# Fetching one gathered tile in eighteen row by row, from SyncE's and ScalarE's queues

## The reference

```python
def _batchnorm(x, gamma, beta):
    mu = jnp.mean(x, axis=0)
    var = jnp.var(x, axis=0)
    return (x - mu) * jax.lax.rsqrt(var + BN_EPS) * gamma + beta

def _gin_conv(x, src, dst, n, W1, b1, gamma, beta, W2, b2):
    agg = jax.ops.segment_sum(x[src], dst, num_segments=n)
    h = x + agg
    h = jax.nn.relu(_batchnorm(h @ W1 + b1, gamma, beta))
    return jax.nn.relu(h @ W2 + b2)
...
h = jnp.maximum(_layernorm(x, axis=-1), 0.0)      # the input of the network
h = _batchnorm(h, g0, b0)
h = _gin_conv(h, src, dst, n, W1a, b1a, g1, bt1, W1b, b1b)
h = jax.nn.relu(h)
h = _gin_conv(h, src, dst, n, W2a, b2a, g2, bt2, W2b, b2b)
return x + jax.nn.relu(h)
```

## Time and profile before

| | |
|---|---|
| median of 3 runs | 3099.09 us (3087.79 to 3099.72) |
| the profiled execution, its time | 3089.35 us |
| its span, first to last instruction | 3087.5 us |
| PE busy | 2466.4 us, 80% |
| POOL busy | 1827.8 us, 59% |
| DVE busy | 1767.5 us, 57% |
| ACT busy | 450.5 us, 15% |
| gathers on POOL | 1908, 946 ns each |
| mean granted TensorE clock | 0.925 |

### The profile page before, as it was taken

How to read it: one execution, slowest core, us unless ns; L and a number is a source line. 1 busy time by engine, 2 the same in 40 slices (tenths; PEclk the granted TensorE clock), 3 DMA queues, 4 the chain that set the end, 5 groups by cost and what they waited for, 6 DMA issues and landing times.

```text
span 3087.5 us, 30879 instructions
## 1 busy us (share of the span) xinstructions
PE 2466.4 (80%) x10965; PEld 1989.1 (64%) x10965; DVE 1767.5 (57%) x3146; ACT 450.5 (15%) x1311; POOL 1827.8 (59%) x1931
## 2 busy tenths in 40 slices
PE   0086007999999999999998969988888888888888
PEld 0085006777777777777776738877777676777766
DVE  5999984554555444555545745554444444444457
ACT  8745004000000000000002930000000000000037
POOL 2000007777777777777773077777777777777730
PEclk8557558999999999999999969999999999999999
DMA  6582007777777777777774999877777777777758
GB/s 209 186 276 63 0 0 239 247 249 248 252 252 250 246 248 248 248 252 252 248 248 157 328 280 320 302 247 247 248 249 252 251 248 247 248 248 250 252 189 255
DMA packets 262079, 716.17 MB, mean 232 GB/s; under 512 B 38334, under 2 KB 129098, under 8 KB 261918
## 3 DMA queue, kind: packets, MB, share of 16 engines
q0 software_dynamic: 159424, 592.77, 59.3%
q1 hardware_dynamic: 102494, 121.33, 12.1%
HBM read 621.27 MB, written 92.69 MB: 231 GB/s over the span
## 4 chain that ended last, share of the span: by engine, by line
PE 43%; DMA 24%; DVE 15%; POOL 10%; issue 6%; ACT 1%; SPq 0%; DVEq 0%; ACTq 0%; POOLq 0%
PE agg_ps L655 36%; DMA rows<-node_rows,src_all 22%; POOL rows L573 10%; DVE work L1022 5%; DVE work L1023 5%; PE mm_ps L697 3%; PE mm_ps L779 2%; PE mm_ps L701 2%; DMA rows<-in_x 1%; ACT acc L889 1%; DVE work L1452 1%; DVE acc L1458 0%; DMA work<-in_src 0%; PE tr_ps L680 0%; DVE rows L1066 0%
## 5 line engine op out<-in xcount | busy, mean ns | idle before, releaser
L573 POOL DMA_INDIRECT rows<-node_rows,src_all x1908 | 1805.8, 946 | 1128.8 <-issue 545.4
L655 PE MATMUL agg_ps<-rows,work 128*128 128x257 f32 (+1 forms) x8056 | 1874.1, 387 | 243.3 <-DMA rows<-node_rows,src_all 239.3
L655 PEld LDWEIGHTS agg_ps<-rows,work 128*128 128x128 f32 x8056 | 1501.8, 191 | 593.3 <-DMA rows<-node_rows,src_all 220.0
L1291 DVE SCALAR_TENSOR_TENSOR acc<-agg_ps,in_first,acc 128x256 f32 (+1 forms) x230 | 111.5, 485 | 1185.2 <-PE agg_ps L655 1182.9
L1236 DVE TENSOR_TENSOR work<-code_all,lane_ps 128x1536 f32<-128x1536 f32 x212 | 369.7, 1744 | 1.1 <-issue 1.1
L845 ACT ACTIVATE bn_root<-bn_var 128x2 f32<-128x2 f32 x3 | 0.6, 200 | 2300.7 <-DVE bn_var L1202 2300.7
L697 PE MATMUL mm_ps<-sum_major,w_a 128*128 128x256 f32 x784 | 198.5, 386 | 2.1 <-DVE sum_major L1306 1.3
L779 PE MATMUL mm_ps<-w_b,work 128*128 128x256 f32 x784 | 176.4, 387 | 28.0 <-ACT work L901 17.4
L779 PEld LDWEIGHTS mm_ps<-w_b,work 128*128 128x128 f32 x784 | 139.9, 193 | 64.5 <-ACT work L901 30.6
L697 PEld LDWEIGHTS mm_ps<-sum_major,w_a 128*128 128x128 f32 x784 | 144.7, 190 | 36.6 <-issue 16.3
L901 ACT ACTIVATE work<-acc,bn_shift,bn_scale 128x128 f32<-128x128 f32 x392 | 165.8, 484 | 15.2 <-PE mm_ps L779 11.2
(11 more groups left out here) (235 smaller groups left out, 1376.8 us busy)
## 6 DMA issues: line engine op xcount, KB each, us to landing
node_rows<-acc SPq DMA_DIRECT2D x141, 260.0 KB, 4.7
rows<-node_rows,src_all POOLq DMA_INDIRECT x1908, 4.4
node_rows<-acc SPq DMA_DIRECT2D x27, 910.0 KB, 4.1
node_rows<-acc SPq DMA_DIRECT2D x126, 130.0 KB, 4.3
acc<-in_x SPq DMA_DIRECT2D x13, 896.0 KB, 11.0
rows<-in_x SPq DMA_DIRECT2D x13, 896.0 KB, 7.1
out<-acc SPq DMA_DIRECT2D x13, 896.0 KB
acc<-in_x SPq DMA_DIRECT2D x1, 768.0 KB
```

Of the source, the lines that this page charges most:

```text
L573: pool.indirect_dma_start(tile_rows(k, 0, ROWS_OF[t] * DP), None, tables[layer][0:NPOS if layer and g < TWICE and t >= LAST_PAIRED else TA ...
L655: mm = pe.matmul(bank[:, 0:width], hot[:, unit * P:(unit + 1) * P], tile_rows(k, row, width), start=(start and n == 0), stop=(stop and n = ...
L1291: dve.scalar_tensor_tensor(to, agg_ps[g % 2][:, 0:width], lanes[:, g:g + 1], to, ALU.mult, ALU.add).then_inc(sums_added, 1)
```

## The change

In every second edge row (the odd ones, from row 7 in layer 0 and from row 19 in layer 1) tile 8 is no longer gathered by POOL. It is fetched by 128 DMAs of one table row each: lanes 0 to 63 are issued by SP, lanes 64 to 127 by ACT. That is 50 tiles in layer 0 and 44 in layer 1. Each DMA is preceded by the loading of its row number into a register from the new buffer `row_src`, in which DVE stores the numbers of tile 8 at set-up (one operation more). Before the first DMA of a tile the queue waits, as POOL does, for `tiles_done`. The fetched tiles are counted in four semaphores of their own, `row_landed`; the gathered ones use the 24 as before, numbered among themselves. The placing of tiles and the order of PE's and DVE's work are unchanged.

```diff
+ROW_TILE = T - 1
+FIRST_BY_ROWS = 7
+QUEUE_ROWS = P // 2
+ROW_LANDINGS = 4
+
+def by_rows(layer, g, t):
+    return t == ROW_TILE and g % 2 == 1 and g >= (TWICE if layer else FIRST_BY_ROWS)
...
+GATHERED = [k for k, tile in enumerate(TILES) if not by_rows(*tile)]
+FETCHED = [k for k, tile in enumerate(TILES) if by_rows(*tile)]
+GATHER_OF = {k: n for n, k in enumerate(GATHERED)}
+FETCH_OF = {k: n for n, k in enumerate(FETCHED)}
...
+        row_src = sb("row_src", [P, P], I32)
...
+        def wait_landed(engine, k):
+
+            if k in FETCH_OF:
+                n = FETCH_OF[k]
+                engine.wait_ge(row_landed[n % ROW_LANDINGS], 16 * P * (n // ROW_LANDINGS + 1))
+            else:
+                n = GATHER_OF[k]
+                engine.wait_ge(tile_landed[n % LANDINGS], 16 * (n // LANDINGS + 1))
...
+            def fetch_rows(layer):
+
+                sp.wait_ge(walk_ready, 1)
+                sp.wait_ge(first_stored, FIRST_DMAS[layer])
+                sp.wait_ge(table_stored, TABLE_DMAS[layer])
+                for k in FETCHED:
+                    if TILES[k][0] == layer:
+                        g = TILES[k][1]
+                        sp.wait_ge(tiles_done, TILE_BEFORE[k] + 1)
+                        for lane in range(0 * QUEUE_ROWS, (0 + 1) * QUEUE_ROWS):
+                            place = sp.value_load(row_src[g:g + 1, lane:lane + 1], min_val=0, max_val=NPOS - 1)
+                            sp.dma_start(rows[lane:lane + 1, TILE_AT[k] * DP:(TILE_AT[k] + 1) * DP],
+                                         tables[layer][bass.ds(place, 1), :]
+                                         ).then_inc(row_landed[FETCH_OF[k] % ROW_LANDINGS], 16)
+
+            fetch_rows(0)
             copies = copies_of(1)
...
             for to, of, stored in copies:
                 sp.dma_start(to, of).then_inc(stored, 16)
+            fetch_rows(1)
             sp.wait_ge(walks_done, 2)
...
                     for t in tiles_of(layer, g):
-                        gather(layer, g, t)
+                        if not by_rows(layer, g, t):
+                            gather(layer, g, t)
...
                     k = NUMBER[layer, g, t]
-                    pe.wait_ge(tile_landed[k % LANDINGS], landed(k))
+                    wait_landed(pe, k)
...
             def dense(layer):
                 add_self(layer)
                 if layer == 0:
                     bn_root_of(0)
                     act.wait_ge(consts_loaded, 16 * CONST_DMAS)
+                fetch_rows(layer)
                 bn_root_of(layer + 1)
...
+            step(dve.tensor_scalar(row_src[:, :], place_ints[:, ROW_TILE * P:(ROW_TILE + 1) * P], -float(UP), NPOS - 1.0,
+                                   ALU.add, ALU.min))
```

More of the change, by code:

```diff
@@ L306, in build @@
         tile_landed = [sem(f"tile_landed{i}") for i in range(LANDINGS)]
+        row_landed = [sem(f"row_landed{i}") for i in range(ROW_LANDINGS)]
         hot_begun = sem("hot_begun")
@@ L372, in tile_rows, with last_users @@
             return rows[:, at_row:at_row + width]
[L374 to L378, removed]
+        def wait_landed(engine, k):
[5 more added lines that the diff above has]
+                engine.wait_ge(tile_landed[n % LANDINGS], 16 * (n // LANDINGS + 1))
+        def last_users(layer):
+            own = [k for k in GATHERED if k < (layer + 1) * NT][-LANDINGS:]
+            return own + [k for k in FETCHED if k < (layer + 1) * NT][-ROW_LANDINGS:]
         def by_tile(of, tiles):
@@ L575, in gather @@
                     bass.IndirectOffsetOnAxis(src_all[:, g * T + t:g * T + t + 1], 0)
[L576 removed]
+                ).then_inc(tile_landed[GATHER_OF[k] % LANDINGS], 16)
             for layer in range(2):
@@ L587, in _ @@
                     for t in tiles_of(layer, g):
-                        gather(layer, g, t)
-            for i in range(LANDINGS):
-                pool.wait_ge(tile_landed[i], last_landed(1, i))
+                        if not by_rows(layer, g, t):
+                            gather(layer, g, t)
+            for k in last_users(1):
+                wait_landed(pool, k)
         @block.tensor
@@ L889, in add_self, with fetch_rows @@
                     act.activation(to, to, ACT.Identity, scale=self_scale[:, 0:1]).then_inc(self_added, 1)
+            def fetch_rows(layer):
+                act.wait_ge(walk_ready, 1)
+                act.wait_ge(first_stored, FIRST_DMAS[layer])
+                act.wait_ge(table_stored, TABLE_DMAS[layer])
+                for k in FETCHED:
+                    if TILES[k][0] == layer:
+                        g = TILES[k][1]
+                        act.wait_ge(tiles_done, TILE_BEFORE[k] + 1)
+                        for lane in range(1 * QUEUE_ROWS, (1 + 1) * QUEUE_ROWS):
+                            place = act.value_load(row_src[g:g + 1, lane:lane + 1], min_val=0, max_val=NPOS - 1)
+                            act.dma_start(rows[lane:lane + 1, TILE_AT[k] * DP:(TILE_AT[k] + 1) * DP],
+                                         tables[layer][bass.ds(place, 1), :]
+                                         ).then_inc(row_landed[FETCH_OF[k] % ROW_LANDINGS], 16)
             def dense(layer):
@@ L1382, in walk @@
                     dve.wait_ge(self_added, (layer + 1) * NB)
-                    for i in range(LANDINGS):
-                        dve.wait_ge(tile_landed[i], last_landed(layer, i))
+                    for k in last_users(layer):
+                        wait_landed(dve, k)
                     for q in range(D // QUARTER):
```

## The result

| | before | after |
|---|---|---|
| median | 3099.15 us (3087.79 to 3099.72, 4 runs) | 9882.81 us (9879.25 to 9885.66, 4 runs) |
| ratio | | 3.192, 95% interval 3.187 to 3.197 |
| span of the profiled execution | 3087.5 us | 9877.4 us |
| mean granted TensorE clock | 0.925 | 0.623 |

The kernel became 3.2 times slower. The prediction said 8100 us with a range from 6800 to 10,500: the direction, the mechanism and the range held, and the likeliest value was 18% too low.

The account below looks back on a forecast made before the run. POOL's issuing of one gather every 1.25 us was taken to bound the kernel. Remainder 984.5, fetches 6317, loops 790 and last landings 6 gave a span of 8098 us, with 1.9 around it 8100 us; range 6800 to 10,500.

Parts of the forecast that it names:

- What bounds the kernel: In the walks, POOL's issue of one gather every 1.25 us sets the pace; removing 94 saves at most 118 us.
- The waits: the loop through the ring: A fetch waits for the tile that held its ring place, usually one row before, so 67 us a tile can't be hidden.
- The 13 tiles with the older holder: Fetched tiles whose ring place was held by tile 2 of two rows before; the queue goes straight on, E = 0.
- E: Time outside the fetch in each loop (landing, matmuls, pair work, clock, semaphores): 10 us, 79 times, 790 us.
- The queues: SyncE and ScalarE work side by side, ScalarE at SyncE's price, so a tile costs 64 c = 67 us.
- The price c: One row's fetch on a queue's sequencer: load and check 0.66, address 0.10, DMA issue 0.29, together 1.05 us.
- Rival 1: On the fetching queues, nobody waits for the load's answer, its 0.30 us vanish: c = 0.75, 6300 us; chance 8%.
- Rival 2: DMA issue on the two queues is dearer, by mutual blocking or the register address: c = 1.43, 10,400 us; chance 8%.
- Rival 3: A load costs 0.6 us on the two fetching sequencers: c = 1.35, 9900 us; chance 7%.
- Rival 4: One-row DMAs of a queue land one after the other, 2.2 us each: 141 us a tile, 15,000 us; chance 3%.
- Rival 5: The two queues keep ahead of PE and POOL's relief comes through: some 110 us less, 2990 us; chance 2%.
- its deciding point: At PE's wait for tile 8, queues keep ahead if 64 c + 8 = 22.5, c = 0.23 us.

Follow-up runs that it names:

- experiment 6: Changed kernel with the 94 tiles neither gathered nor fetched (PE multiplies what lies in their places): 2973.7 us, ratio 0.962 to the kernel before.
- experiment 5: Changed kernel with the fetched tiles landing in four places of their own outside the ring, waiting only for the fetched tile four before: 9063 us.
- experiments 3, 4, 7: Changed kernel with only SyncE's 64 rows fetched: 9288 us; with only ScalarE's: 9841 us; with 66 lanes by SyncE and 62 by ScalarE: 9644 us.
- experiment 2: Changed kernel with the loads in groups of four, each group ahead of its four DMAs, same instructions: 8051 us.
- experiment 4: Changed kernel with only ScalarE's 64 rows of each tile fetched, SyncE issuing none: 9841 us.
- experiment 1: Changed kernel with a constant row number in each DMA, so no load, register operations, assertion or address: 4272 us.
- experiments 8 to 10: Against the kernel before: every sixth, fifth, fourth row's tile 8 fetched, own places, sixteen loads before DMAs, last two without bounds check: 0.989, 0.987, 0.982.

## Why the prediction was right, and where it was off

*What bounds the kernel.* Right. POOL's 1.25 us a gather sets the pace; experiment 6 gives 116 us for 94 gathers, 1.23 each.

*The waits: the loop through the ring.* Right, and shown by cutting it (experiment 5). The 13 tiles with the older holder follow on without a pause, and no others do. Its size was forecast too large: 9877.4 - 984.5 - 6 - 6016 x 1.372 leaves 633 us for 79 turns, so E = 8.0 us and not 10, as in experiment 5. The part that was off is the landing: PE restarts 0.9 us on average behind the end of the last issue (0.8 in the loop shown), where 2.2 for landing and 0.8 for semaphores had been added. The rest, PE's work from its restart to the next fetch, was taken at 7.0 us (14 matmuls, pair work, 2 for the clock) and measures 7.1. The clock's share in it was read from a single restart, and single restarts differ, as the stages above show. Here is a full edge row after a wait, beside the 8.4 us for 38 matmuls of the earlier trace rows:

```profile
1015.37 10.94 PE L699 MATMUL agg_ps<-rows,work 128*128 128x257 f32 x38
```

PE's busy time rose from 2466 to 2672 us, near the 190 us foreseen. PE's waits were forecast at 50 to 55 us and are 72 on average, because the fetches in their shadow are dearer.

*The queues.* The two work side by side without touching each other: right (experiments 3, 4, 7). That they cost the same was taken from SyncE's rows for want of any of ScalarE's, and was wrong: 9841 us against 9288.

*The price c, the term that was mis-sized.* It was taken at 1.05 us; ScalarE's measured 1.372 and SyncE's 1.269. The mechanism stood, only this size was off: 6016 x 0.322 is 1940 us too little. The 2 us too much in each of 79 E's, 160 us, hid a part of it, and the remaining 1780 us are the whole miss from 8098 to 9877 us of span. Piece by piece on ScalarE: the load 0.48 us instead of 0.31; the operations 0.152, as forecast; the DMA 0.45 instead of 0.24; and a register MOVE of 29 ns that was not counted (a fetch is six instructions in the trace, not five). These make 0.41, of which about 0.1 comes back because the address (0.042 for 0.057) and the gaps had been priced too high; the three long steps of a tile add 0.02. What failed is the step that took each duration from a row in which the instruction stood among others of its own kind or none at all: VectorE's load, which no DMA precedes, and SyncE's L441, three issues in a row. Experiment 2 gives that step its due: with loads behind loads and DMAs behind DMAs about the prices taken come out, 0.27 to 0.28 and 0.21 to 0.23 us, a fetch takes 1.03 us, and the time (8051 us) stands next to the forecast one. The alternation makes the rest. A small slip besides: layer 1's replaced stretch starts by its own row at 1991.5 and not 1991.7, 0.2 us of the sum.

*The rivals.* Rival 1 (the load hidden, 6300 us) is false: the operations begin 0.5 us after the load's start, when it is over. Rival 2 (issuing dearer, c = 1.43) had half the truth, a DMA of 0.45 us on ScalarE. Of its two reasons, two queues that block each other are refuted by experiment 4, and the register address by experiment 2, where ScalarE's DMAs with such an address take 0.21 us behind one another. Rival 3 gave 9900 us, within 0.2% of the result, and that is luck: its load of 0.60 us measures 0.48 to 0.50, the DMA makes up for what is missing, and its E of 10 us is 8. The Trainium skill's floor of about 600 ns for a `tensor_load` ("DMA: Bandwidth & Descriptors", section "Latency and other measured facts") is undercut by every median here: 0.30 us on VectorE, 0.28 in a run of loads, 0.48 to 0.50 right behind a DMA, and 0.53 to 0.57 for the first load behind a group of four DMAs. By that section of the Trainium skill the compiler's unrolling by four amortizes it, and four at a time is indeed cheaper (experiment 2), though each load still stands in line. Rival 4 is false at this pace and begins to show in experiment 1. Rival 5 is false for every second edge row, and its deciding point is what experiments 8 to 10 meet by asking for less.

*Open.* Why the change between a load and a DMA costs what it does, and why ScalarE pays about 0.24 us for the DMA and SyncE 0.035, isn't settled; experiment 2 shows only that the cost sits at the change. Nor is it known what limits the landing to a row in 0.23 us in experiment 1: not the row transfers' own time alone, but the trace doesn't tell which of the 16 DMA engines carried a row, nor what it did besides.

## What to carry to other kernels

An idle engine's queue is not a free DMA issuer. Count what its sequencer runs for each descriptor (load, check, address, issue), price it in the order in which it will run, and set elements x price against the stretch that must hide it; here 64 x 1.37 = 88 us stood against 22.5. Where row numbers must be loaded, put many loads ahead of many DMAs, and give what is fetched slowly a buffer of its own, so that it doesn't wait for the fast ring. Price the issue and the loop around it apart, or an error in one can hide in the other. Then hand over just as much as is hidden: 45 of 1908 gathers in place of 94 turned a factor of 3.2 into a gain of 1.8%.

## What the runs showed of the hardware that was not expected

- A register load takes 0.28 us behind another load and 0.48 to 0.57 behind a DMA issue, on SyncE and ScalarE alike (experiment 2).
- A one-row DMA with its address in a register takes ScalarE's sequencer 0.45 us behind a load's operations and 0.21 behind another DMA; SyncE's takes 0.26 to 0.27 and 0.225 (experiment 2).
- One-row DMAs of 1040 bytes, issued at 0.16 us a row by two queues together, landed at about 0.23 us a row (experiment 1); at 0.69 us a row the last one landed 0.8 us behind its issue.
- PE came back at half its clock behind all 94 waits of 61 to 75 us, and had the full clock 2.8 to 25 us later, 5.0 in the median (the changed kernel).
